# Mamba and feed-forward block on one core: for every second transposed unit, ScalarE makes all four token blocks of the scaled copies, and GpSimd none

## What is computed

```python
def step(h, inp):
    xt, dtt, Bt, Ct = inp
    dA = jnp.exp(dtt[:, :, None] * A)
    h = dA * h + (dtt * xt)[:, :, None] * Bt[:, None, :]
    y = jnp.einsum('ben,bn->be', h, Ct)
    return (h, y)
```

## Time and profile before

| | us |
|---|---|
| median of 3 runs (12999.0 to 13004.58) | 12999.88 |
| the profiled execution | 13003.51 |
| its span in the trace | 13001.7 |

### The profile page before, as it was taken

One profiled execution on the slowest core, in us unless ns is written; L12 is line 12 of the kernel. 1 busy time (PEld: TensorE's weight loads), 2 busy tenths in 40 slices (PEclk: granted clock), 3 DMA queues, 4 the chain that ended last, 5 costly groups with the idle time before them and its releaser, 6 DMA issues.

```text
span 13001.7 us, 179153 instructions
## 1 busy us (share of the span) xinstructions
PE 10179.6 (78%) x51228; PEld 5796.2 (45%) x51228; DVE 12010.2 (92%) x7080; ACT 10850.5 (83%) x23452; POOL 11539.1 (89%) x5988
## 2 busy tenths in 40 slices
PE   5667877788787887878878787887878878778777
PEld 2334544444444444544445444444444445444445
DVE  5999999999999999999999999999999999999992
ACT  5788888888888898888888888888888988888883
POOL 4899999999999999999999999899999999999992
PEclk7788988889898898988989888898989989889898
DMA  2223333333333333333333333333333333333332
GB/s 83 83 84 109 118 108 123 119 105 115 109 126 109 114 121 102 125 110 118 118 109 116 107 124 118 107 115 108 124 110 115 120 104 127 108 118 117 110 109 96
DMA packets 605385, 1450.11 MB, mean 112 GB/s; under 512 B 68400, under 2 KB 109504, under 8 KB 599792
## 3 DMA queue, kind: packets, MB, share of 16 engines
q1 hardware_dynamic: 604272, 1437.26, 33.9%
HBM read 1346.70 MB, written 90.31 MB: 111 GB/s over the span
## 4 chain that ended last, share of the span: by engine, by line
PE 28%; ACT 23%; issue 21%; DVE 16%; POOL 11%; DMA 1%; DVEq 0%; SPq 0%; POOLq 0%; ACTq 0%
DVE state L1242 10%; PE driven L867 9%; POOL state L1272 8%; ACT state L1054 8%; ACT v_sb L1067 8%; PE y_ps L881 5%; PE q_ps L822 4%; DVE driven L1231 3%; PE q_ps L809 2%; PE p_ps L730 2%; PE b_ps L857 2%; ACT L1054 1%; POOL v_sb L1347 1%; PE p_ps L738 1%; PE p_ps L754 1%
## 5 line engine op out<-in xcount | busy, mean ns | idle before, releaser
L1272 POOL TENSOR_TENSOR state<-state,c_rep 128x1024 f32<-128x1024 f32 x4096 | 9671.1, 2385 | 1050.9 <-DVE state L1242 1048.4
L1242 DVE TENSOR_TENSOR_SCAN state<-state,driven 128x1024 f32<-128x1024 f32 x4096 | 9107.5, 2271 | 512.9 <-PE driven L867 313.4
L1054 ACT ACTIVATE state<-ud_rep,cols_sb 128x512 f32<-128x512 f32 x8192 | 5180.4, 709 | 2.2
L1067 ACT ACTIVATE v_sb<-u_t,b_t 128x128 f32<-128x128 f32 x12288 | 3980.1, 505 | 1190.3 <-PE driven L867 1186.0
L867 PE MATMUL driven<-consts_sb,v_sb 128*128 128x128 f32 x16384 | 2638.2, 314 | 1636.0 <-DVE state L1242 1602.1
L867 PEld LDWEIGHTS driven<-consts_sb,v_sb 128*128 128x128 f32 x16384 | 2133.9, 161 | 3279.2 <-DVE state L1242 2196.2
L881 PE MATMUL y_ps<-state,consts_sb 128*32 128x512 f32 x16384 | 2492.0, 684 | 511.2 <-POOL state L1272 508.4
L1231 DVE TENSOR_TENSOR driven<-ud_rep,b_ps 128x1024 f32<-128x1024 f32 x2048 | 2390.2, 1213 | 16.3 <-DMA ud_rep<-ud_rows 16.3
L822 PE MATMUL q_ps<-hid,wq_sb 128*128 128x256 f32 x7936 | 2061.9, 405 | 191.4 <-ACT hid L1032 124.1
L822 PEld LDWEIGHTS q_ps<-hid,wq_sb 128*128 128x128 f32 x7936 | 1481.5, 196 | 906.7 <-issue 709.3
L1347 POOL TENSOR_TENSOR v_sb<-u_t,b_t 128x512 f32<-128x512 f32 x1024 | 1159.6, 1132 | 13.2 <-ACT u_t L980 13.2
(11 more groups left out here) (139 smaller groups left out, 5543.2 us busy)
## 6 DMA issues: line engine op xcount, KB each, us to landing
c_rep<-bc_rows SPq DMA_DIRECT2D x2048, 256.0 KB, 3.0
ud_rep<-ud_rows SPq DMA_DIRECT2D x512, 512.0 KB, 4.0
wq_sb<-in_h SPq DMA_DIRECT2D x512, 512.0 KB, 3.8
wq_sb<-in_f SPq DMA_DIRECT2D x128, 512.0 KB, 4.1
wp_sb<-in_win SPq DMA_DIRECT2D x64, 512.0 KB, 4.5
dt_sb<-conv_taps SPq DMA_DIRECT2D x32, 1024.0 KB, 5.7
ud_rows<-u_pad SPq DMA_DIRECT2D x128, 256.0 KB, 3.5
ud_rows<-dt_sb SPq DMA_DIRECT2D x128, 256.0 KB, 3.4
```

What stands on the lines that cost most here:

```text
L1054: ins = act.activation(state[:, unit % STATE_RING, j, :], ud_rep[:, nth % 2, j, 1, :], ACT.Exp, scale=a_neg[:, d, c, j, g:g + 1])
L1067: ins = act.activation(v_sb[:, unit // 2 % V_RING, tt, :, :, n].rearrange("p j e -> p (j e)"), u_t[:, nth % 2, tt, :], ACT.Identity, scale ...
L1242: dve.tensor_tensor_scan(flat, flat, driven[:, q % DRIVE_RING].rearrange("p j t -> p (j t)"), 0.0, ALU.mult, ALU.add).then_inc(scanned, 1)
L1272: pool.tensor_tensor(part, part, c_rep[:, unit % ROW_RING, :].unsqueeze(1).to_broadcast([P, 2, T]), ALU.mult).then_inc(was_read, 1)
```

## The change

`pooled(unit)` is true for the odd units 1, 5, 9, ... (unit % 4 == 1) and false for 3, 7, 11, .... For the pooled ones nothing changes. For the others GpSimd's multiplication is gone, and ScalarE makes block 3 as well, by four more activations at the head of part 1. The counts of `v_pooled` are halved wherever somebody waits for them, and TensorE doesn't wait for `v_pooled` ahead of a unit that has none.

```diff
+        def pooled(unit):
+
+            return unit % 4 == 1
...
                 if h == 0:
                     pe.wait_ge(v_made, v_count(at, unit))
-                    pe.wait_ge(v_pooled, v_count(at, unit))
+                    if pooled(unit):
+                        pe.wait_ge(v_pooled, of_body(at, len(PE_UNITS) // 2, unit // 4 + 1))
...
-                        act.wait_ge(v_pooled, of_body(at, len(PE_UNITS), NG // 2 * (nth - 1)))
+                        act.wait_ge(v_pooled, of_body(at, len(PE_UNITS) // 2, NG // 4 * (nth - 1)))
...
-                for tt in (2, 1) if part else (0,):
+                for tt in ((2, 1) if pooled(unit) else (3, 2, 1)) if part else (0,):
                     for n in range(NN):
                         ins = act.activation(v_sb[:, unit // 2 % V_RING, tt, :, :, n].rearrange("p j e -> p (j e)"),
...
             def make_v(at, unit):
                 nth, g = unit % UNITS // NG, unit % NG
+                if not pooled(unit):
+                    return
                 pool.wait_ge(pe_driven, v_free(at, unit))
```

More of the change, by code:

```diff
@@ L975, in step @@
                         if at.kind != "pre" and not (d and at.kind == "first"):
-                            act.wait_ge(v_pooled, of_body(at, len(PE_UNITS), 0 if d else len(PE_UNITS) // 2))
+                            act.wait_ge(v_pooled, of_body(at, len(PE_UNITS) // 2, 0 if d else len(PE_UNITS) // 4))
                         act.activation(b_t[:, d].rearrange("p a n -> p (a n)"), p_ps[:, 0:TT * N], ACT.Copy).then_inc(done, 1)
```

## The result

The changed kernel takes 13140.28 us (4 runs, 13131.61 to 13142.0) against 13002.23 us of the kernel before: 1.0103 times as long, 95% interval 1.0087 to 1.0119, or +138 us. Forecast were +150 us.

A forecast was written before the change was run, and what follows sets the result against it. ScalarE was taken as the bound by turns, for some 200 us of each 788 us body. 160 + 30 - 40 = +150 us on 12999.88 gives 13150 us, 1.2% slower, range 13050 to 13300.

The forecast's parts named there:

- ScalarE's price: 2048 added activations, 599 us of work: 160 us on the chain that ended last, 30 in blocks with little slack.
- GpSimd's relief: 512 multiplications dropped from GpSimd: 65 us lie on the chain, 40 us taken as gain, bounds 0 and 98.
- The lines of VectorE with two inputs: VectorE's addition at L1218, slowed by something near it: less GpSimd work gains below 10 us, costed at nothing.
- The first rival: The added work hides in ScalarE's waits ahead of the copies: 12960 to 13020 us; chance 7%.
- The second rival: GpSimd held the end, with copies ahead of its reads on the chain: faster, 12,935 us; chance 7%.
- The third: ScalarE becomes the bound nearly everywhere, half or more of the 512 blocks count: 13300 to 13600 us; chance 8%.
- What the next profile would show: ScalarE busy about 11450 us, GpSimd 10960; waits ahead of copies fall; ScalarE-full stretches grow about 1.17 us per four units.

The follow-up runs named there:

- both halves: Two runs against the kernel before: ScalarE's four copies added with GpSimd's multiplication kept, 13160.7 us; GpSimd's multiplication dropped and made by nobody, 12945.49 us.
- the light blocks: Changed kernel, but ScalarE makes all four blocks only for 13 units per body where it was busy at most about 80%; 13000.99 us, ratio 1.0003.
- the run that lengthens only the heavy units: Changed kernel, but ScalarE makes all four blocks only for the other 19 units of a body, GpSimd block 3 for the rest; 13158.7 us, ratio 1.0126.

## Why the prediction was right

**ScalarE's price, taken as 160 on the chain and 30 near it:** alone it measures 166 us, and that holds the 30 us or so which L1212 gives back. Without them it is some 196 us, so both parts, 190 together, were about right. By the table ScalarE's work alone adds 12.0 us per body outside units 40 to 44, 192 in 16 bodies.

**GpSimd's relief, taken as 40 of the 65 on the chain:** alone it measures 50, inside the bounds of 0 and 98. But again some 30 of them are L1212's, so GpSimd's place on the chain was worth about 20 by the medians (the profiled execution, 12 us below its median, has 2.5 us per body outside units 40 to 44, or 40).

**The lines of VectorE with two inputs, taken as nothing, below 10 us:** this step failed. VectorE is busy for 46 us less in the changed kernel (12010.2 to 11964.2), 40 of them at L1212 (128.6 to 88.9 us), and the bodies of the kernel before put a price of some 30 us on its long instances. I had looked at L1218 alone and priced it by GpSimd's load; with GpSimd's load unchanged L1212 falls as well, to 88.8 us. The 1.8 us that units 40 to 44 give back are there in both halves. The Trainium skill (SBUF — State Buffer, section Who interferes with whom) calls the port pair that VectorE and GpSimd share an exclusive lock, and has the order of issue decide who blocks. The trace agrees with the lock: 62 of 64 instances end 2.15 us behind an instruction of GpSimd. The order of issue alone doesn't give the ten long ones, in which two more instructions of GpSimd, both shown as beginning after VectorE's, went ahead of it. What decides that is not shown here.

**The closeness of +150 to +138 is partly luck:** by the medians GpSimd's relief was taken 20 us too high, and the 30 us of L1212 were left out.

**Work, not place:** I priced an activation alike in part 0 and in part 1. By the run with block 3 in part 0 this is wrong by some 55 of 138 us, for a reason that is open for the most part. One candidate was in the profile before: of the 227 us of ScalarE's idle time at the evacuation some 170 lie between the two parts (the rest is one wait per body, at its end).

**The first rival,** that ScalarE's idle time hides the work, held where it had idle time: the light blocks cost nothing. ScalarE as a whole had 2151 us to spare and the change is 138 us slower, so the occupancy rule of the Trainium skill (Perfetto Trace Analysis, section Identifying the Most-Contended Engine) doesn't decide this case: work went from an engine at 89% to one at 83% and the time rose. **The second rival** asked for fewer than 55 blocks that count. At 1.17 us, 166 us are 142 blocks. **The third** asked for 300 us and more; measured were 138.

**What the next profile would show:** ScalarE's 14336 activations are there, and it is busy for 11423 us (11450 forecast), GpSimd for 10991 (10960). The waits for decays rose by 186 us (over 100), the waits at the copies fell. The heavy stretches grew by 4.0, 2.3 and 3.1 us, where 1.17 us for four units make 4.7, 2.3 and 2.3. Units 44 to 104 grew by 2.3 us as well, by the heavy places among them: the run that lengthens only the heavy units has 359.7 us there, the one with the light units 356.1, against 356.5 before. The granted clock went from 0.885 to 0.879 in the profiled executions; the forecast had no term for it.

## What to carry to other kernels

To price work added to an engine that is not full, take the share that its present instructions of the same kind have in the chain, and check it stretch by stretch: here 25% of the copies lay on the chain, and the added work cost 28% of its 599 us, or some 33% without what L1212 gave back. Moving work between engines pays by place, not by mean load: the same block cost 0.54 us in one set of units and nothing that can be told in the other. Look at what stands between two halves of a movable block: with eight copies ahead of the evacuation in place of four the kernel was 65 us faster, as much as by any shift of work between engines. And before you put a gain down to the edit, see by stretch where it lies: about half of these 65 us is one instruction of VectorE that happened to meet GpSimd at a better moment, and every one of the faster kernels has that gain, in all or nearly all of its bodies.

## What the hardware showed that I had not expected

The same VectorE instruction (128x2048 f32, two inputs in SBUF) took 4020 ns in the mean in one kernel and 2774 ns in another that differs by four activations of ScalarE in every second block, with GpSimd's work the same; in one run of the kernel before it reached from 2293 to 6524 ns, and it ended 2.15 us behind the end of an instruction of GpSimd in all but one of its 32 instances. And an activation of 128x128 costs 0.29 us behind another one, though each is shown with 0.50 us.
